# The row lists of the last routed batch: a table in memory replaced by one-hot products

## The reference

```python
logits = x @ gate_weight.T
logits = jnp.where(old_to_new[None, :] == -1, -jnp.inf, logits)   # 48 of 128 experts are kept
probs = jax.nn.softmax(logits, axis=-1)
top_v, top_i = jax.lax.top_k(probs, 8)
top_v = top_v / jnp.sum(top_v, axis=-1, keepdims=True)
flat_e, flat_w = old_to_new[top_i].reshape(-1), top_v.reshape(-1)
oh = (flat_e[:, None] == jnp.arange(48)[None, :]).astype(jnp.int32)
pos = jnp.sum(jnp.cumsum(oh, axis=0) * oh, axis=-1) - 1
valid = pos < 192                                                  # each expert takes 192 tokens at most
xb = zeros(48, 192 + 1, 512).at[flat_e, where(valid, pos, 192)].set(x[tok])
g, u = split(einsum('ech,eoh->eco', xb[:, :192], gate_up_proj))
out = einsum('eci,ehi->ech', silu(g) * u, down_proj)
final = zeros_like(x).at[tok].add(out[flat_e, pos] * (flat_w * valid)[:, None])
```

## Time and profile before

| | |
|---|---|
| median of 3 runs | 2161.02 us |
| lowest and highest | 2158.72 and 2165.73 us |
| the profiled execution's own time | 2160.38 us |
| its span, first to last instruction | 2158.7 us |
| busy share of the span | PE 81%, DVE 71%, POOL 50%, ACT 44% |
| mean granted clock of TensorE | 0.891 of full speed |

### The profile page before, as it was taken

How to read it: one execution, slowest core, us unless ns; L and a number is a source line. 1 busy time by engine, 2 the same in 40 slices (tenths; PEclk the granted TensorE clock), 3 DMA queues, 4 the chain that set the end, 5 groups by cost and what they waited for, 6 DMA issues and landing times. The chain is left out here.

```text
span 2158.7 us, 34592 instructions
## 1 busy us (share of the span) xinstructions
PE 1740.1 (81%) x9155; PEld 1385.4 (64%) x9156; DVE 1525.7 (71%) x2891; ACT 956.8 (44%) x1867; POOL 1073.2 (50%) x809
## 2 busy tenths in 40 slices
PE   4898988457999999999998888787832079999990
PEld 3566564246889888888886555555421068888880
DVE  4467776755877878887874324788879757777774
ACT  4355453212444444444442334445423157777773
POOL 1000633664667666676675000054528647777761
PEclk9899999657999999999999898888865589999995
DMA  8011111045888898888896513131010369999967
GB/s 324 26 40 59 38 42 40 1 128 158 206 212 208 213 225 213 218 224 225 218 235 160 158 19 59 59 59 59 1 59 20 129 188 256 256 251 257 257 153 254
DMA packets 138552, 318.80 MB, mean 148 GB/s; under 512 B 30712, under 2 KB 31320, under 8 KB 136824
## 3 DMA queue, kind: packets, MB, share of 16 engines
q1 hardware_dynamic: 71448, 201.74, 27.1%
q0 software_dynamic: 64752, 112.04, 26.9%
q10 hardware_dynamic: 2288, 4.29, 0.5%
HBM read 238.68 MB, written 97.62 MB: 156 GB/s over the span
## 5 line engine op out<-in xcount | busy, mean ns | idle before, releaser
L98 POOL DMA_INDIRECT tab_rows<-pair,slot x256 | 314.5, 1229 | 451.8 <-DVEq L752 292.0
L90 PE MATMUL gu<-wgu_h,xgT_h 128*128 x648 | 233.8, 361 | 7.3 <-DVE xgT_l L1428 3.6
L1253 POOL DMA_INDIRECT xg<-x_rows,ids x167 | 191.7, 1148 | 64.1 <-issue 48.5
L90 PE MATMUL gu<-wgu_l,xgT_h 128*128 x648 | 219.7, 339 | 0.0
L90 PE MATMUL gu<-wgu_h,xgT_l 128*128 x648 | 218.5, 337 | 0.0
L1308 ACT ACTIVATE ysb<-yp,wts 128x512 f32<-128x512 f32 x160 | 110.1, 688 | 144.0 <-PE yp L1535 144.0
L90 PE MATMUL guk<-xgT_hk,wgu_hk 128*128 128x192 f32 x576 | 161.2, 280 | 0.0
L90 PE MATMUL guk<-xgT_lk,wgu_hk 128*128 128x192 f32 x576 | 158.3, 275 | 0.0
L90 PE MATMUL guk<-xgT_hk,wgu_lk 128*128 128x192 f32 x576 | 158.3, 275 | 0.0
L1298 ACT ACTIVATE sg<-gu 128x192 f32<-128x192 f32 x162 | 53.6, 331 | 235.3 <-PE gu L90 235.3
L1428 DVE TENSOR_TENSOR xgT_l<-tpx,xgT_h 128x512 fp32r<-128x512 f32 x163 | 112.1, 688 | 55.0 <-ACT xgT_h L1294 52.9
(11 more groups left out here) (501 smaller groups left out, 5037.4 us busy)
## 6 DMA issues: line engine op xcount, KB each, us to landing
wgu_sb<-in_wgu SPq DMA_DIRECT2D x64, 768.0 KB
wgu_sbk<-in_wgu SPq DMA_DIRECT2D x48, 768.0 KB, 4.4
wd_sb<-in_wd SPq DMA_DIRECT2D x64, 256.0 KB
wd_sbk<-in_wd SPq DMA_DIRECT2D x48, 256.0 KB, 5.2
ct<-in_ctxT SPq DMA_DIRECT2D x8, 1024.0 KB, 4.9
wd_sb<-in_wd SPq DMA_DIRECT2D x64, 128.0 KB
wd_sbk<-in_wd SPq DMA_DIRECT2D x48, 128.0 KB, 5.8
odd_rows<-zero SPq DMA_DIRECT2D x1, 4352.0 KB, 15.5
```

The lines of the kernel that those rows point to most:

```text
L90: i = nc.tensor.matmul(out, left(k), right(k), start=(start and k == 0 and m == 0), stop=(k == ops - 1 and m == 2))
L98: nc.gpsimd.indirect_dma_start(out=tab, out_offset=bass.IndirectOffsetOnAxis(ap=s["slot"][:, n:n + 1].bitcast(U32), axis=0), in_=s["pair"] ...
L1253: nc.gpsimd.indirect_dma_start(out=xg[:, t % G, :], out_offset=None, in_=x, in_offset=bass.IndirectOffsetOnAxis(ap=ids[:, t:t + 1].bitcast ...
```

## The change

The last batch is routed at once like the others, and its pairs don't go through the table.

- The table, which then holds batches 0 to 2, is loaded by SP within `mixer_two`, once their scatters have landed, into the free buffer `x3`. VectorE waits for this load at the start of `drained` and makes the token numbers float.
- `route_rows` runs once over four tiles, and the fourteen position products run together.
- `parts_made` builds five bf16 numbers for each pair and expert: the one-hot `hot` itself, `hot` times the token number, and `hot` times the weight in three parts whose sum is the full weight. `spots_made` builds, for each pair, a one-hot over the 192 positions.
- TensorE sums over the 128 partitions and all 32 pairs: 64 products of the position one-hot (128 or 64 columns of weights) with the 240 numbers (5 × 48), into two banks. In front of them it transposes the loaded table.
- `lists_taken` adds the two: the table's entry is padding where the new batch fills the slot, and the sum corrects it. It writes `ids` and `wts`, which now live outside both blocks.
- The scatters of the last batch are gone, 32 indirect DMAs. In `kept_experts` the table's load, its transposes and copies are gone. The gather buffer is cleared in four pieces, each with its own signal, and the first expert's copies and splits of rows are queued ahead of the casts and subtractions of the weights, which start with the block.
- The counts `macc1` are no longer updated after the last batch.

```diff
 def kept_experts(nc, d, s):
@@ gpsimd
-            scatter(nc, tab, s, E1 * REG1 - 1, s_lot, BT - 1)
...
             def gather(t):
                 if t >= GK:
                     pool.wait_ge(s_xT, t - GK + 1)
+                elif t % 2 == 0:
+                    pool.wait_ge(s_clear, t // 2 + 1)
...
-            pool.wait_ge(s_tab, 3)
@@ scalar
             for n in range(2):
+                copy_xT(0, n)
                 gate_up_upper(0, n, False)
                 down_upper(0, n, False)
-            act.wait_ge(s_lot, SCAT)
-            nc.scalar.dma_start(lot[:, :, :].rearrange("t n o -> t (n o)"),
-                                tab.rearrange("(r n) o -> r (n o)", n=P)[0:T1, :]).then_inc(s_rows, 16)
-            copy_xT(0, 0)
-            copy_xT(0, 1)
@@ vector
-            nc.vector.memset(xg[:, :, :], 0.0).then_inc(s_tab, 1)
+            for n in range(NF):
+                nc.vector.memset(xg[:, 2 * n:2 * n + 2, :], 0.0).then_inc(s_clear, 1)
...
             for n in range(2):
+                split_xT(0, n)
                 gate_up_lower(0, n)
                 down_lower(0, n)
-            dve.wait_ge(s_rows, 16)
-            c.done(nc.vector.tensor_copy(lotf[:, :], lot[:, :, 0]))
-            c.wait()
...
 def mixer_two(nc, d, s):
@@ sync
+                    else:
+                        sp.wait_ge(s_scat, (B - 1) * (16 * BT * TOPK))
+                        sp.wait_ge(s_rin, 2 * B * BT)
+                        sp.wait_ge(s_xT, B * KC)
+                        sp.dma_start(lot.rearrange("t n o -> t (n o)"),
+                                     d["tab1"].rearrange("(r n) o -> r (n o)", n=P)[0:T1, :]).then_inc(s_lot, 16)
                     sp.wait_ge(s_x5, b * BT + BT)
@@ gpsimd
-            for j in range(BT - 1):
-                pool.wait_ge(s_idx, B + j + 1)
-                settle(pool, passed)
-                scatter(nc, d["tab1"], drain, E1 * REG1 - 1, s["lot"][1], j, j + 1)
...
+            pool.wait_ge(s_scat, (B - 1) * (16 * BT * TOPK))
@@ vector, drained
                 c.done(nc.vector.tensor_scalar(tokf[:, :], tokf[:, :], float(S), None, ALU.add))
+                c.done(nc.vector.tensor_scalar(back[:, :], s["tcol"][:, 0:1], -1.0, -float(2 * P), ALU.mult, ALU.add))
+                dve.wait_ge(s_lot, 16)
+                c.done(nc.vector.tensor_copy(lotf, lot[:, :, 0]))
                 dve.wait_ge(s_x4, B * BT)
...
+                def parts_made():
+                    wf, rest = ok, en
+                    dve.wait_ge(s_ex, (B - 1) + (ROUTED + 1))
+                    c.done(nc.vector.tensor_reduce(esum[:, :], ex8[:, :, :], AX.X, ALU.add))
+                    c.done(nc.vector.tensor_scalar(tok16[:, :], tokf[:, :], -float(TOK - 2 * P), None, ALU.add))
+                    c.wait()
+                    c.done(nc.vector.reciprocal(esum[:, :], esum[:, :]))
+                    c.done(nc.vector.tensor_tensor(parts[:, 1, :, :].rearrange("p e (j k) -> p e j k", k=TOPK),
+                                                   own.rearrange("p e (j k) -> p e j k", k=TOPK),
+                                                   tok16[:, :].unsqueeze(1).unsqueeze(3).to_broadcast([P, E1, BT, TOPK]), ALU.mult))
...
+                    c.done(nc.vector.tensor_tensor(parts[:, 2:5, :, :], own.unsqueeze(1).to_broadcast([P, 3, E1, NP]),
+                                                   w16[:, :, :].unsqueeze(2).to_broadcast([P, 3, E1, NP]), ALU.mult))
+                def spots_made():
+                    dve.wait_ge(s_pos, (B - 1) + (ROUTED + 1))
...
+                    for n in range(0, NP, NP // 2):
+                        for m, (lo, w) in enumerate(((0, P), (P, IR))):
+                            nc.vector.tensor_tensor(spots[:, lo:lo + w, n:n + NP // 2], iota16[:, 0:w, 0:NP // 2],
+                                                    at16[:, m, n:n + NP // 2].unsqueeze(1).to_broadcast([P, w, NP // 2]),
+                                                    ALU.is_equal).then_inc(s_spot, 1)
+                def lists_taken():
+                    dve.wait_ge(s_list, 1)
...
-                for j in range(BT):
-                    route_j(j)
-                    slots_j(j)
...
+                routed()
+                parts_made()
+                spots_made()
+                lists_taken()
@@ tensor, drained
+                nc.tensor.transpose(tp[:, 0, 0:T1], lotf, ident[0:T1, 0:T1])
+                nc.tensor.transpose(tp[:, 1, 0:T1], lot[:, :, 1].bitcast(F32), ident[0:T1, 0:T1])
+                for n in range(NP):
+                    if n % (NP // 2) == 0:
+                        pe.wait_ge(s_spot, n // (NP // 2) * 2 + 2)
+                    for m, (lo, w) in enumerate(((0, P), (P, IR))):
+                        i = nc.tensor.matmul(tb[0:w, m, 0:5 * E1].rearrange("p (v e) -> p v e", e=E1), spots[:, lo:lo + w, n],
+                                             parts[:, :, :, n], start=(n == 0), stop=(n == NP - 1))
+                i.then_inc(s_list, 1)
```

More of the change, by code:

```diff
@@ L1932, in mixer_two @@
         ok = sb("ok3", [P, BT * TOPK])
-        drain = dict(slot=sb("slot3", [P, BT * TOPK], I32), pair=sb("pair3", [P, BT * TOPK, 2], I32))
+        NP = BT * TOPK
+        spots = vres[:, :, :, :].rearrange("p a j n -> p (a j n)").bitcast(BF16)[:, 0:CAP * NP].rearrange("p (r n) -> p r n", n=NP)
+        parts = scans[:, :, :, :].rearrange("p a k n -> p (a k n)").bitcast(BF16)[:, 0:5 * E1 * NP].rearrange("p (v e n) -> p v e n", v=5, n=NP)
+        ids, wts = s["ids"], s["wts"]
+        lot = x3[0:T1, 0, 0:2 * P].bitcast(I32).rearrange("t (n o) -> t n o", o=2)
+        lotf = x3[0:T1, 1, 0:P]
+        tok16 = sb("tok163", [P, BT], BF16)
+        w16 = sb("w163", [P, 3, NP], BF16)
+        at16 = sb("at163", [P, 2, NP], BF16)
+        back = sb("back3", [P, 1])
+        idf = sb("idf3", [P, 2, 2, E1])
         spare = sb("spare3", [P, 1])
@@ L1946, in mixer_two @@
         s_wi, s_w = s["weights"]
+        s_lot = s["lot"][1]
+        s_spot = sem("spots_ready")
+        s_list = sem("lists_product")
         s_set = sem("constants_set")
@@ L2448, in route @@
                 dve.wait_ge(s_lg, b + (ROUTED + 1))
-                yield from route_rows(c, range(BT), lgp, 0)
+                yield from route_rows(c, range(BT), lgp, hot)
                 assert c.n == KRT, c.n
@@ new lines, in lists_taken @@
+                def lists_taken():
+                    dve.wait_ge(s_list, 1)
+                    half = []
+                    for m, rows in ((0, slice(0, P)), (1, slice(0, IR))):
+                        there = tb[rows, m, 0:5 * E1].rearrange("p (v e) -> p v e", e=E1)
+                        early = [tp[rows, n, 0:T1].rearrange("p (e h) -> p e h", h=2)[:, :, m] for n in range(2)]
+                        out = [t[rows, :].rearrange("p (e h) -> p e h", h=2)[:, :, m] for t in (ids, wts)]
+                        half.append((there, early, out, idf[rows, m, 0, :], idf[rows, m, 1, :], back[rows, 0:1]))
+                    for there, _, _, f, g, b in half:
+                        c.done(nc.vector.tensor_scalar(f, there[:, 0, :], b, None, ALU.mult))
+                        c.done(nc.vector.tensor_copy(g, there[:, 3, :]))
+                    c.wait()
+                    for there, _, _, f, g, _ in half:
+                        c.done(nc.vector.tensor_tensor(f, f, there[:, 1, :], ALU.add))
+                        c.done(nc.vector.tensor_tensor(g, g, there[:, 4, :], ALU.add))
+                    c.wait()
+                    for there, early, out, f, g, _ in half:
+                        c.done(nc.vector.tensor_tensor(out[0], f, early[0], ALU.add))
+                        c.done(nc.vector.tensor_tensor(g, g, there[:, 2, :], ALU.add))
+                    c.wait()
+                    for _, early, out, _, g, _ in half:
+                        c.done(nc.vector.tensor_tensor(out[1], g, early[1], ALU.add))
+                    c.wait()
@@ L2518, in drained @@
                 scaled(3)
-                for j in range(BT):
-                    route_j(j)
-                    slots_j(j)
-                with nc.allow_low_precision("small counts"):
-                    for j in range(BT):
-                        c.done(nc.vector.tensor_tensor(s["macc1"][:, :], s["macc1"][:, :], mask[:, j, :], ALU.add))
-                        c.wait()
+                routed()
+                parts_made()
+                spots_made()
+                lists_taken()
             norm1(0, True)
```

98 lines of the change are left out of this document (44 added, 54 removed).

## The result

The changed kernel takes 2195.68 us, the median of 4 runs (2193.76 to 2197.61), against 2163.38 for the kernel before in the same comparison (4 runs, 2158.72 to 2167.86). The ratio is 1.0147, with a 95% interval of 1.0123 to 1.0171: slower by 32 us. The forecast was 2181, with a range up to 2192. The direction was right, the size too small, and the time lies above the range. The profiled execution took 2194.96 us, its span is 2193.2, 34.5 more than before, at a mean granted clock of 0.884.

What follows compares the result with a forecast made beforehand. TensorE was taken to bound the experts' stage, with a serial stretch ahead: 20.4 us early wait, 5.1 waiting for logits, 2.3 clearing, 2.6 experts' start, less 10.1 saved, give +20.3 on the 2158.7 span; forecast 2181 us, range 2162 to 2192.

Steps and rivals of the forecast that it cites:

- The early wait: In `drained`, VectorE waits for the table load before its first add: a stall of 20.4 us.
- Rows to logits: Last batch, from the first add to the end of the fourth logits: unchanged, 15.0 us.
- `parts_made`, positions, first spots: VectorE before the products: number parts 6.0 us, position product and reduction 4.5 plus 0.3 for copies, first comparisons 1.8.
- Lists: `lists_taken` on VectorE, fourteen operations on 48 columns: 2.0 us and 0.3 for the hand-over.
- The 64 products: TensorE's products with strided columns at 1.67 ns each: 0.40 us a product at either clock, 25.6 us in all.
- rival 3: In the 64 products, the weights' loads are exposed too: 35.9 us, +30.6, total 2191.6; chance 0.09.
- The experts' start: First gather to first down product: 22.5 us against 19.9, so +2.6, bounds 0 and 6.
- The experts' stage: 1760 to 2100 us: bound by TensorE, busy 328 of 340 us; its start carries over to the end one for one.
- the other pace that the prediction named as a sign of being wrong: Sign against the forecast: the experts' stage running at another pace than TensorE busy 328 us in 340.
- the first (strided columns are free): In the 64 products, strided columns cost TensorE nothing: 8.9 us in place of 25.6, +3.6, total 2164.6; chance 0.25.
- the second (half the price): In the 64 products, the step costs 0.83 ns a column: 12.8 us, +7.5, total 2168.5; chance 0.16.
- the fourth: The wait in `drained` is short or absent and strided columns are free: −16.8 us, total 2144; chance 0.04.

Runs made afterwards that it cites:

- Run 5: Changed kernel with VectorE's wait for the table and its copy moved behind the token and weight parts, transposes right before the products: 2183.53 us, ratio 1.0088.
- run 1: Changed kernel plus 208 idle products of 240 columns behind the 64, for six steps of the moving operand and six of the weights: 2246.87 us.
- run 9: Changed kernel with pairs layout (columns 2 elements apart), late table wait and products ordered by width: ratio 0.9983, repeated 0.9979.
- run 2: Changed kernel plus two sets of nine groups of 16 idle products, varying weight widths, banks, steps, shifts and an open sum: 2310.58 and 2275.01 us.
- run 3: Changed kernel with the same 64 products reordered, the 32 wide ones first, one-hots compared in that order: ratio 1.0115, products 26.62 us.
- Run 7: Changed kernel with SP waiting for the first two gathers' landing before issuing the second expert's weights: 2195.66 us, ratio 1.0147.
- run 8: Changed kernel with pairs layout and late table wait: ratio 1.0068; also with expert 0's gating ahead of expert 2's weights on ScalarE and VectorE: 1.0064.
- run 6: The changed kernel again, unaltered: 2198.69 us, ratio 1.0159.

## Why the prediction fell short

- **The early wait** (20.4 forecast): 19.3 us net of the 1.4 that stood there before. The chain was as told: last scatter 1667.28, load issued 1669.38, copy at 1671.37. Run 5 shows that it was on the path.
- **Rows to logits** (15.0): 14.2. **Routing at once** (14.6): 14.6. **`parts_made`, positions, first spots** (6.0 + 4.9 + 1.8 = 12.7): 12.6, from 1700.2 to 1712.84. The mixed form with the repeated operand took 1.73 us, as taken, and not the 0.96 of bf16 alone. **Lists** (2.3): 2.2; from there to the first gather 2.6 against 3.2. Two slips in the sum cost 0.3 us at most: its own terms put the table's landing at 1678.8 and not 1679.1, and between VectorE and GpSimd has 0.9 and not 0.8.
- **The 64 products** (25.6): 35.9. This is the step that failed. "I take 25.6 ... if the weights, at the same rate, are exposed too, it is 35.9 us": that value was rival 3 with a chance of 0.09. Its number was met, and its reason only in part. The column rate of 1.67 ns was right (run 1). With one width, the load of the weights was hidden at every step tried (runs 1 and 9); 0.14 us a product came on top because widths alternated (runs 2 and 3), which the prediction never looked at. All rows are of one width. What it costs, 0.14 us, is close to the 0.16 for a mean of 96 rows at 1.67 ns, but with contiguous weights it is still 0.11 (0.509 less 0.403), so the step is at most a small part of it. The Trainium skill's "TensorEngine Tiling (Array Packing)" ("Key Properties") says that changing the tiling mode, 128×128 or 128×64 among them, drains TensorE. The sweeps agree in that each change costs and a change of bank or of operand doesn't; the 512-column products of the kernel before, which change width at 0.228 us, show no price for it. Whether the sweeps' products pay for a drain (TensorE empties before it goes on) or for a load of weights that is no longer hidden stays open, and no run tried 96 columns against 128.
- **The experts' start** (+2.6, bounds 0 to 6): +7.1, beyond its bounds. The sum counted the casts on ScalarE and VectorE and had the rows turned 6 us after the first gather; they were turned after 9.5, which is 3.5 of the 4.5 us that it missed. What it left out is that the weights of experts 1 and 2 load beside the gathers: expert 1's land by 1765.7, when SP asks for expert 3's, for which it waits until then, 14 us after the block's start, and expert 2's at 1772.13, just ahead of ScalarE's cast at 1772.15, behind which the gating stood. Run 7 takes the competition from the gathers and run 8 the order from the queues; neither gives time, so the loads are the likely bound. With the lists ready at 1750.95 and the loads beginning at 1751.51, what was once hidden under the scatters lies open.
- **The experts' stage**: nothing forecast, +8.9 us. In the kernel before all intervals were 7.7 us and the stretch from the first down product to the end 404 us; in the five profiles of a changed kernel beside 2161 to 2163 us it was 407 to 413, with stalls of 0.4 to 5 us, at different experts each time. TensorE's 322 us of 340 (322 in run 6 too) are the other pace that the prediction named as a sign of being wrong. The stage is not bound by TensorE alone, as the prediction had it, but also by gathers that land just in time. Why they land about 1 us later in the changed kernels (6.0 us, from the quarter of the landings that the trace has; 5.4 to 6.5 in the four others) isn't settled; the kernel before was profiled once, and may have such stalls in other executions.
- **Luck**: −6.8 us in the profiled execution, ahead of the change. The three other parts add up to 41 us, and the medians differ by 32: some 9 us of the profiles' difference are not in the medians, and which part they belong to isn't known. It is by such sums, too, that the total came so near rival 3's +30.6: that rival had nothing for the stage and 2.6 for the start.

The sum in the profile: 17.7 forecast to the first gather, 25.2 measured (10.3 more for the products, 2.8 less in the terms above); 2.6 and 7.1 for the start; 0 and 8.9 for the stage; less 6.8: +34.5 on the span.

Of the rivals, the first (strided columns are free) and the second (half the price) are out by run 1, the fourth by the stall. Half the price does exist, at a step of 4 elements and the 2.4 GHz level.

## What to carry to other kernels

Lay out a small matrix product so that its columns lie at most 2 bf16 elements apart and so that products of one width follow each other: here that is 9.5 us against 35.9 for the same 64 products of 240 columns; in products of 512 columns on f32 data the change of width was free. When a load through memory is moved forward, put the wait for it at its first use, not at the head of the stage. When the work that hid the next stage's weight loads is taken away, those loads lie open and slow what runs beside them: here the first rows were turned 9.5 us after their gather, 4.5 before.

## What was unexpected of the hardware

- A moving operand of bf16 at a step costs by what lies in 16 bytes: 240 columns take 0.103 us at steps up to 2 (0.20 at the 1.2 GHz level), 0.21 at 4 (2.4 GHz level), and 0.40 to 0.43 at 8, 16 and 32, where the clock makes no difference. At the 1.2 GHz level a step of 4 costs nothing more than one of 2 (0.372 and 0.369 with widths in turn). That fits one 16-byte stretch every 1.67 ns, an inference from these six steps. The Trainium skill's "SBUF — State Buffer" ("Door 1: The DMA port swizzle") names 16-byte lines and full bandwidth with two hits a line, bf16 free up to a step of 8. The runs agree on the size of the line; they differ on what is free: at the 2.4 GHz level two in a line (step 4) already take twice the time, and step 8 four times; at the 1.2 GHz level step 4 is free and step 8 takes twice the time.
- The stationary operand at a 64-byte step costs TensorE at most 0.01 us a product (0.112 against 0.103), as long as widths don't change.
- Between bf16 products of 240 columns, a change between 128 and 64 columns of weights costs 0.11 to 0.17 us, as much as a whole product of 240 contiguous columns (0.103 at the 2.4 GHz level). Between products of 512 columns on f32 data it costs nothing that shows (0.228 us from start to start).
